# Decays of a Mamba-2 layer: four row-grouped exponents instead of six, y between the projections, past decays as a product, squares on ScalarE

## The chip, the cores and the metric

One core of a Trainium2 chip. The metric is the device time of one execution in microseconds (us), lower is better.

## The reference

A Mamba-2 mixer and a quantised feed-forward layer, both with a layer norm before and a residual after, over 4 x 256 tokens of width 512 in float32. Cut to what matters here:

```python
proj = einsum('bsd,ed->bse', x, in_proj_w)      # gate, hBC, dt
hBC = silu(conv4(hBC) + conv_b)                 # hs (128 heads x 64), B and C (8 groups x 128)
dt = clip(softplus(dt + dt_bias), 0, 100); A_dt = -exp(A_log) * dt
# two chunks of 128 tokens for each batch; A_cum is the cumulative sum of A_dt in a chunk
L = exp(segsum(A_dt))                           # own decays, below the diagonal
Y_diag = (C B^T * L) @ (hs * dt)                # inside a chunk
states = B^T (exp(A_cum_last - A_cum) * hs * dt)
Y_off = C @ prev_state * exp(A_cum)             # second chunk from the first
y = Y_diag + Y_off + hs * D
g = y * silu(gate); g = g * rsqrt(mean(g * g in its group) + eps) * norm_w
x = x + g @ out_proj_w.T
x = x + ffn(layernorm(x))                       # 1792 hidden, quantised activations
```

## The kernel before

Engines run their own programs and meet at semaphores; the order of the work on each is written out by hand. Matmuls that must be exact in float32 are split into high and low parts and done in three (`three`, L758 to L760).

**Outer order.** A prologue (norm of x, transposes, the projection of dt, softplus, cumulative sums, the first tile's and group's projections), then 8 groups of 8 tiles. A tile is two heads (128 channels) over all 1024 tokens. After the 8 tiles of a group comes a window: the B and C projections of the next group, the sum of squares, 16 blocks of out projection (L945 to L947) that are added to the residual, and the products of C and B (`cbs`, L840 to L842), kept masked in `cb`. The feed-forward layer follows.

**A step.** The step of tile t also makes the projections of tile t+1. On TensorE: transposes of half of `hs` (`turn`, L858), the exponents of two of six decay blocks (L867), `unit(0)` (12 matmuls of 128x512), the other transposes, two exponents, `unit(1)`, the first part of y (`y_first`, L881), the last two exponents, `unit(2)`, `unit(3)`, and `y_second` (L891). The blocks are: inside chunk 0, chunk 0 to chunk 1, and inside chunk 1, for each of two heads. An exponent is one bf16 matmul over 128 partitions, of which 15 hold rows (three parts of each cumulative sum, and marks); the rest are zeros.

ScalarE turns a block into a decay: for a block inside a chunk Relu and Exp in place in PSUM (L640, L644), for the past one Exp (L634). It also does the last tap of the convolution (`tap3`, L558), the tanhs (`hs_tanh` L569, `gate_tanh` L573), the scaling and upper part of the out weights (L666, L672), and the upper parts of the projection weights (L536).

VectorE multiplies decays by `cb` into `M` (`weigh`, L1163), turned hs by dt into `xdt` (`times_dt`, L1155), does the other three taps (`conv_rest`, L1068), the silus (L1082, L1087) and adds y (L1189). A projection bank comes free (`taken`) after `conv_rest` or after the gate's silu.

GpSimd makes the lower parts of weights (L406, L430), y times gate (`gated`, L438), its squares (L447; on ScalarE only in the very last tile, L679) and their sum (L452).

The SyncE queue loads, in each step and in this order, the out weights `wo_raw`, the rows of the next tile's exponents (four transfers) and the projection weights of the tile three pairs ahead (`load_pair`).

Of the kernel before, what the change touches and what calls it, by code (L numbers as in the profile page):

```python
# [12 lines left out]
P = 128  # L13
# [16 lines left out]
UNITS = 6  # L30
SLOT = [0, 1, 2, 3, 0, 1]
# [18 lines left out]
def over_tiles(eng, step, window):  # L50


    with eng.Fori(0, G - 1) as g:
        with eng.Fori(0, TPG // 2) as p:
            step(g, 2 * p, 0, True, True)
            step(g, 2 * p + 1, 1, True, True)
        window(g, True)
    with eng.Fori(0, TPG // 2 - 1) as p:
        step(G - 1, 2 * p, 0, True, True)
        step(G - 1, 2 * p + 1, 1, True, True)  # L60
    step(G - 1, TPG - 2, 0, True, False)
    step(G - 1, TPG - 1, 1, False, False)
    window(G - 1, False)
# [12 lines left out]
def mamba_ffn(nc, x, win, wdt, par, parbc, dt_bias, a_log, wout, w1, w3, w2, s1, s3, s2, out):  # L76
    rows_r = nc.dram_tensor("rows_r", (3, H, TOK), BF16, kind="Internal").ap()
    rows_l = nc.dram_tensor("rows_l", (3, B, H, 3, P), BF16, kind="Internal").ap()

    with ExitStack() as ctx:  # L80
# [23 lines left out]
        M = sb("M", [P, 4, HALF])  # L104
        bc = M[:, :, :].rearrange("p (a u) f -> p a (u f)", a=2)
# [3 lines left out]
        row_r = sb("row_r", [P, 2, 2, TOK], BF16)  # L109
        row_l = sb("row_l", [P, 2, 2, 3 * P], BF16)  # L110
        sq = sb("sq", [P, 2, HALF])
        after, bias_bc, nega_bc = [sq[:, 0, i * P:(i + 1) * P] for i in range(3)]
# [12 lines left out]
        qs = sb("qs", [P, 2, 4])  # L125
        qr = sb("qr", [P, 2, 4])
# [9 lines left out]
        rev, revrem = dte[:, 0:HALF], dte[:, HALF:TOK]  # L136
        r_part = flat[:, 4 * TOK:6 * TOK].bitcast(BF16)[:, 0:3 * TOK].rearrange("p (k f) -> p k f", k=3)
        neg_part = flat[:, 6 * TOK:8 * TOK].bitcast(BF16)[:, 0:3 * TOK].rearrange("p (k f) -> p k f", k=3)
        rev_part = pre[0].bitcast(BF16)[:, 0:3 * HALF].rearrange("p (k f) -> p k f", k=3)
# [3 lines left out]
        f_pair = M[:, :, :].rearrange("p k (w f) -> p w k f", w=2)  # L143
# [21 lines left out]
        diff = [bank("diff0"), bank("diff1")]  # L165
        ybank = [bank("y0"), bank("y1")]
        trb = bank("trb")
        misc = bank("misc")
        xbank = proj + diff
        nbank = [trb, misc]  # L170
        dbank = diff + [misc]
# [17 lines left out]
        s_held_p = sem("held_pool")  # L189
# [14 lines left out]
        s_part = [sem(f"exact_part{k}") for k in range(3)]  # L204
        s_rest = sem("rest_of_parts")
        s_rows = sem("rows_stored")
        s_raw = [sem("w_raw0_loaded"), sem("w_raw1_loaded")]
        s_rowq = [sem("rows_even_loaded"), sem("rows_odd_loaded")]
        s_out = sem("out_stored")
# [10 lines left out]
        turned = Tally(sem("hs_transposed"), 0, 2)  # L220
        xdts = Tally(sem("xdt_done"), 1, 2)
        dready = Tally(sem("diff_ready"), 0, UNITS)
        dbound = Tally(sem("diff_bounded"), 0, 4)
        edone = Tally(sem("exp_done"), 0, UNITS)
        mdone = Tally(sem("decay_done"), 3, UNITS)
        yready = Tally(sem("y_ready"), 1, 3)
# [47 lines left out]
        def _(sp):  # L274
# [12 lines left out]
            for n in range(3):  # L287
                load_pair(n, 2 * n if n else None)

            def load_rows(t, par_):  # L290
                sp.dma_start(row_r[0:3, par_, :, :], rows_r[:, bass.ds(2 * t, 2), :]).then_inc(s_rowq[par_], 16)
                for k in range(3):
                    sp.dma_start(row_l[3 + 4 * k:7 + 4 * k, par_, :, :].rearrange("b h f -> b (h f)"),
                                 rows_l[k, :, bass.ds(2 * t, 2), :, :].rearrange("b h q f -> b (h q f)"))\
                        .then_inc(s_rowq[par_], 16)


            for k in range(3):
                sp.wait_ge(s_part[k], 3)
                sp.dma_start(rows_r[k, :, :], r_part[:, k, :]).then_inc(s_rows, 16)  # L300
                sp.dma_start(rows_l[k, :, :, 1, :].rearrange("b h l -> h b l"),
                             rev_part[:, k, :].rearrange("h (b l) -> h b l", b=B)).then_inc(s_rows, 16)
                for z in range(2):
                    sp.dma_start(rows_l[k, :, :, 2 * z, :].rearrange("b h l -> h b l"),
                                 neg_part[:, k, :].rearrange("h (b z l) -> h z b l", z=2, b=B)[:, z, :, :])\
                        .then_inc(s_rows, 16)
            sp.wait_ge(s_const, 13)
            sp.dma_start(row_r[3:15, 0, 1, :], row_r[3:15, 0, 0, :]).then_inc(s_marks, 16)
            sp.dma_start(row_r[3:15, 1, 0, :], row_r[3:15, 0, 0, :]).then_inc(s_marks, 16)
            sp.dma_start(row_r[3:15, 1, 1, :], row_r[3:15, 0, 0, :]).then_inc(s_marks, 16)  # L310
            sp.wait_ge(s_rows, 16 * 12)
            load_rows(0, 0)

            def step(g, j, par_, nxt, nxt2):
# [39 lines left out]
        def _(pool):  # L354
# [18 lines left out]
            e.memset(row_r[:, :, :, :], 0.0).then_inc(s_const, 1)  # L373
            e.memset(row_l[:, :, :, :], 0.0).then_inc(s_const, 1)
            pool.wait_ge(s_const, 9)
            e.memset(row_l[0:3, :, :, :], 1.0).then_inc(s_const, 1)
            columns = row_r[:, 0, 0, :].rearrange("p (b f) -> p b f", b=B)
            for k in range(3):
                pool.wait_ge(s_const, 10 + k)
                e.affine_select(out=columns, in_=columns, compare_op=ALU.not_equal, fill=1.0, base=-3 - 4 * k,  # L380
                                pattern=[[-1, B], [0, S]], channel_multiplier=1).then_inc(s_const, 1)
# [31 lines left out]
            split_pair(0, 0)  # L413
            split_pair(1, 2)

            wholes = ((acum, rem, r_part), (rev, revrem, rev_part))
            for i, (whole, rest, parts) in enumerate(wholes):
                pool.wait_ge(s_part[0], i + 1)
                e.tensor_tensor(rest, whole, parts[:, 0, :], ALU.subtract).then_inc(s_rest, 1)
            for i, (whole, rest, parts) in enumerate(wholes):  # L420
                pool.wait_ge(s_rest, i + 1)
                pool.wait_ge(s_part[1], i + 1)
                e.tensor_tensor(parts[:, 2, :], rest, parts[:, 1, :], ALU.subtract).then_inc(s_part[2], 1)
            split_pair(1, 4)

            def step(g, j, par_, nxt, nxt2):
# [15 lines left out]
                for h in range(2 if nxt else 0):  # L442
# [74 lines left out]
        def _(act):  # L517
# [164 lines left out]
            def window(g, nxt):  # L682
# [24 lines left out]
                if not nxt:  # L707
                    x_upper(n2, TT - 3)
# [642 lines left out]
```

## Time and profile before

| | |
|---|---|
| median of 3 runs | 1861.39 us (1861.02 to 1861.64) |
| the profiled execution's own time | 1863.36 us |
| its span in the trace | 1861.6 us |
| granted TensorE clock, mean | 0.986 |
| PE, DVE, POOL, ACT busy | 97%, 67%, 54%, 49% |

PE is TensorE, PEld its weight loads, DVE VectorE, ACT ScalarE, POOL GpSimd. A busy share is that of the span in which at least one instruction of the engine is under way. Matmuls overlap their successors: what one costs in a stream is the distance between starts, not its duration. The same holds, more weakly, for DVE and ACT.

### The profile page before, as it was taken

The page shows a single profiled execution, that of the slowest core. Times are in us where ns is not written, and L with a number is a line of the kernel's source. Part 1 is how long each engine was busy: PE and PEld are TensorE (multiplying, and loading weights), DVE is VectorE, ACT ScalarE, POOL GpSimd, SP SyncE. Part 2 cuts the span into 40 slices and gives each one's busy share as a digit, 9 for nine tenths or more (in the row PEclk, how much of TensorE's full clock was granted, in tenths as well). Part 3 has the DMA queues.
Part 4 walks back from the last instruction along what each step waited for, and adds up shares of the span by engine and source line. Part 5 has one row for each costly group of instructions (what it writes and reads, how often), then busy time and mean ns, then how long its engine had stood idle before and what let it go on. Part 6 is the DMA issues. An engine that isn't in the chain of part 4 may idle for free.

```text
span 1861.6 us, 35838 instructions
## 1 busy us (share of the span) xinstructions
PE 1805.1 (97%) x10520; PEld 1448.8 (78%) x10520; DVE 1256.5 (67%) x2147; ACT 918.5 (49%) x1660; POOL 1006.2 (54%) x812
## 2 busy tenths in 40 slices
PE   5799999999999999999999999999999998999998
PEld 4577887788777877787778777887788776788886
DVE  6588728872887377746884688457754884877776
ACT  4466526652665256635663566346644663222221
POOL 4266645664566446654665366546654657633430
PEclk9899999999999999999999999999999997999999
DMA  2211101110111011101120111001101111111101
GB/s 93 63 53 41 46 3 45 52 52 0 47 53 52 0 47 51 53 0 36 46 64 6 29 53 53 17 29 53 47 23 30 42 35 53 40 52 35 51 17 46
DMA packets 49019, 74.94 MB, mean 40 GB/s; under 512 B 10356, under 2 KB 18676, under 8 KB 48984
## 3 DMA queue, kind: packets, MB, share of 16 engines
q1 hardware_dynamic: 47976, 73.12, 12.9%
q10 hardware_dynamic: 1008, 1.38, 0.2%
q8 instruction: 18, 0.29, 0.1%
q14 instruction: 17, 0.14, 0.0%
HBM read 70.35 MB, written 4.06 MB: 40 GB/s over the span
## 4 chain that ended last, share of the span: by engine, by line
PE 94%; DVE 2%; POOL 1%; issue 1%; ACT 1%; POOLq 0%; DVEq 0%; ACTq 0%
PE proj L758 16%; PE proj L760 16%; PE proj L759 16%; PE y L891 7%; PE y L945 6%; PE y L947 6%; PE y L946 6%; PE y L881 4%; PE trb L858 3%; PE diff L867 3%; PE y L758 2%; PE y L760 2%; PE y L759 2%; PE misc L867 1%; PE misc L931 1%
## 5 line engine op out<-in xcount | busy, mean ns | idle before, releaser
L758 PE MATMUL proj<-xhi,w_hi 128*128 128x512 f32 x1088 | 466.1, 428 | 5.4 <-DVE v L1068 5.4
L760 PE MATMUL proj<-xhi,w_lo 128*128 128x512 f32 x1088 | 426.2, 392 | 0.0
L759 PE MATMUL proj<-xlo,w_hi 128*128 128x512 f32 x1088 | 425.5, 391 | 0.0
L406 POOL TENSOR_TENSOR w_lo<-w_raw,w_hi 128x512 fp32r<-128x512 f32 x144 | 184.1, 1297 | 227.5 <-ACT w_hi L536 227.5
L1068 DVE SCALAR_TENSOR_TENSOR v<-proj,par_sb,v 128x510 f32<-128x510 f32 (+2 forms) x384 | 282.1, 742 | 14.9 <-ACT v L558 11.6
L758 PEld LDWEIGHTS proj<-xhi,w_hi 128*128 128x128 f32 x1088 | 205.0, 188 | 75.5 <-issue 7.9
L462 POOL TENSOR_TENSOR g_lo<-gated,g_hi 128x512 fp32r<-128x512 f32 x128 | 163.8, 1283 | 182.1 <-ACT g_hi L689 182.0
L760 PEld LDWEIGHTS proj<-xhi,w_lo 128*128 128x128 f32 x1088 | 204.8, 188 | 46.5
L759 PEld LDWEIGHTS proj<-xlo,w_hi 128*128 128x128 f32 x1088 | 205.4, 189 | 38.6
L1163 DVE TENSOR_TENSOR M<-diff,cb 128x512 f32<-128x512 f32 x256 | 170.4, 686 | 82.2 <-ACT diff L644 82.2
L945 PE MATMUL y<-wo_hi,g_hi 128*128 128x512 f32 x512 | 202.9, 396 | 4.0 <-POOL g_lo L462 4.0
L430 POOL TENSOR_TENSOR wo_lo<-wo_raw,wo_hi 128x512 f32 (+1 forms) x64 | 81.9, 1279 | 225.1 <-ACT wo_hi L672 225.1
L946 PE MATMUL y<-wo_lo,g_hi 128*128 128x512 f32 x512 | 200.1, 391 | 0.0
L947 PE MATMUL y<-wo_hi,g_lo 128*128 128x512 f32 x512 | 200.0, 391 | 0.0
L689 ACT CAST g_hi<-gated 128x512 fp32r<-128x512 f32 x128 | 78.6, 620 | 233.6 <-PE y L947 233.6
L558 ACT ACTIVATE v<-proj,par_sb 128x512 f32<-128x512 f32 x128 | 99.6, 778 | 188.7 <-PE proj L760 188.7
L1207 DVE SCALAR_TENSOR_TENSOR resid<-y,rg,resid 128x512 f32<-128x512 f32 x64 | 48.0, 750 | 201.3 <-PE y L947 171.5
L640 ACT ACTIVATE diff<-diff 128x512 f32<-128x512 f32 x192 | 105.5, 579 | 138.1 <-PE diff L867 138.1
L438 POOL TENSOR_TENSOR gated<-hs,gate 128x512 f32 (+1 forms) x128 | 162.8, 1295 | 1.6 <-DVE hs L1189 1.6
L452 POOL TENSOR_TENSOR sqacc<-sqacc,sq 128x512 f32<-128x512 f32 x128 | 163.1, 1297 | 0.0
L891 PEld LDWEIGHTS y<-M,xdt 128*64 128x64 f32 x2048 | 112.0, 138 | 25.7 <-issue 22.2
L891 PE MATMUL y<-M,xdt 128*64 128x128 f32 x2048 | 127.6, 278 | 2.5 <-DVE M L1163 2.5
(179 smaller groups left out, 3420.1 us busy)
## 6 DMA issues: line engine op xcount, KB each, us to landing
w_raw<-in_win SPq DMA_DIRECT2D x144, 256.0 KB, 2.7
wo_raw<-in_wout SPq DMA_DIRECT2D x64, 256.0 KB, 2.6
M<-in_w SPq DMA_DIRECT2D x14, 512.0 KB, 3.7
cb<-in_w SPq DMA_DIRECT2D x7, 512.0 KB, 3.4
row_l<-rows_l SPq DMA_DIRECT2D x192, 6.0 KB
out<-resid SPq DMA_DIRECT2D x8, 256.0 KB, 2.0
rows_l<-gated SPq DMA_DIRECT2D x9, 128.0 KB, 2.5
resid<-in_x SPq DMA_DIRECT2D x4, 256.0 KB, 4.7
```

What stands on the lines that cost most here:

```text
L406: e.tensor_tensor(w_lo[:, slot, i, :], w_raw[:, i, :], w_hi[:, slot, i, :].bitcast(F32), ALU.subtract).then_inc(split.sem, 1)
L452: e.tensor_tensor(halves(sqacc, h), halves(sqacc, h), sq[:, h, :], ALU.add)\
L462: e.tensor_tensor(g_lo[:, kk, :, :], gated[:, 4 * kk:4 * kk + 4, t * P:(t + 1) * P], g_hi[:, kk, :, :].bitcast(F32), ALU.subtract).then_in ...
L758: e.matmul(o, hi_l, hi_r, start=first, stop=False)
L759: e.matmul(o, hi_l, lo_r, start=False, stop=False)
L760: return e.matmul(o, lo_l, hi_r, start=False, stop=last)
L891: mm = e.matmul(ybank[b // 2][head * HD:(head + 1) * HD, (b % 2) * S + P:(b % 2 + 1) * S], xdt[:, 2 * b + part, head * HD:(head + 1) * HD] ...
L945: e.matmul(o, g_hi[:, kk, k, :], wo_hi[:, kt, :], start=first, stop=False)
L946: e.matmul(o, g_hi[:, kk, k, :], wo_lo[:, kt, :], start=False, stop=False)
L947: mm = e.matmul(o, g_lo[:, kk, k, :], wo_hi[:, kt, :], start=False, stop=last)
L1068: e.scalar_tensor_tensor(dst[:, :, d:S], src[:, :, 0:S - d], weights(K - 1 - d), dst[:, :, d:S], ALU.mult, ALU.add)\
L1163: e.tensor_tensor(M[:, SLOT[q], :], dbank[q % 3][:, :], cb[:, q // 2, :], ALU.mult)\
```

## The change

- **Exponents.** Four instead of six: only the blocks inside the chunks. Each one's 15 rows of both operands lie in their own group of 32 partitions (0, 32, 64, 96), and each writes its own PSUM bank: `row_r` and `row_l` shrink, and the rows are loaded with eight transfers instead of four. The exponents of tile j+1 are made in step j, behind y; those of a group's first tile in the window.
- **Decays.** `decay[z]` spans two banks, so Relu, Exp and `weigh_own` take both heads at once (128x1024). `trb` and `misc` become the banks of `decay[1]`; hs is turned into the y banks.
- **Past.** Chunk 0 to chunk 1 is a product. exp(A_cum) of the second chunk (`faded`) is made once, and two transfers in each step spread it over the partitions (`fade_l`); GpSimd multiplies it by `cb` (`weigh_past`, 128x1024). exp(A_last - A_cum) times dt (`fade_s`) is made once; `times_dt` multiplies hs by it as well (`xfade`, 128x512).
- **y.** One block of 24 matmuls between `unit(1)` and the exponents; all eight transposes stand in one block.
- **Squares.** On ScalarE in every tile, in one buffer, each half waiting for the sum of the half before; the last gate tanh of a step stands behind them.
- **Prologue.** B and C are projected before hs and gate of tile 0, with all four first units in banks of their own; fewer parts and rows are made; constants are smaller.

```diff
-            step(g, 2 * p, 0, True, True)
+            step(g, 2 * p, 0, True, True, True)
...
+        row_r = sb("row_r", [P, 2, HALF], BF16)
+        row_l = sb("row_l", [P, 2, P], BF16)
+        fade_l = sb("fade_l", [P, 2, HALF])
+        fade_s = sb("fade_s", [P, B, H])
+        xfade = sb("xfade", [P, B, P])
+        sq = sb("sq", [P, HALF])
...
+        decay = [ctx.enter_context(nc.psum_tensor(f"decay{z}", [P, 2 * HALF], F32)) for z in range(2)]
+        diff = [decay[0][:, 0:HALF], decay[0][:, HALF:2 * HALF]]
+        ypair = ctx.enter_context(nc.psum_tensor("y", [P, 2 * HALF], F32))
+        misc, trb = decay[1][:, 0:HALF], decay[1][:, HALF:2 * HALF]
```

SyncE, one step:

```diff
                 if nxt:
-                    sp.wait_ge(dready.sem, dready.at(g, j, 1))
+                    sp.wait_ge(dready.sem, dready.at(g, j, 0))
                     load_rows(TPG * g + j + 1, 1 - par_)
+                    sp.wait_ge(pdone.sem, pdone.at(g, j, 1))
+                    load_fade(TPG * g + j + 1)
```

GpSimd, the constants:

```diff
-            e.memset(row_r[:, :, :, :], 0.0).then_inc(s_const, 1)
-            e.memset(row_l[:, :, :, :], 0.0).then_inc(s_const, 1)
+            e.memset(row_r[0:PARTS + PARTS * B, :, :], 0.0).then_inc(s_const, 1)
+            e.memset(row_l[:, :, :], 1.0).then_inc(s_const, 1)
```

GpSimd, the past decays and the squares:

```diff
+            def weigh_past(g, j):
+                pool.wait_ge(s_fade, (32 * TPG) * g + 32 * j + 32)
+                pool.wait_ge(cbd.sem, cbd.at(g, 0, 0))
+                pool.wait_ge(yready.sem, yready.at(g, j, 0))
+                e.tensor_tensor(M[:, 4:6, :], fade_l[:, :, :], cb[:, 1:2, :].broadcast_to([P, 2, HALF]), ALU.mult)\
+                    .then_inc(pdone.sem, 1)
...
-                for h in range(2 if nxt else 0):
-                    ...
-                    e.tensor_tensor(sq[:, h:h + 1, :], one, one, ALU.mult).then_inc(sqs.sem, 1)
+                if ahead:
+                    weigh_past(g, j + 1)
```

ScalarE, the order of a step after:

```diff
+                if nxt:
+                    tap3(0, w, ready.at(g, j, 1), silu.at(g, j, -1))
+                if nxt2:
+                    upper_pair(par_, 9 * g + j + 3)
+                if nxt:
+                    tap3(1, w, ready.at(g, j, 2), silu.at(g, j, 0))
+                    hs_tanh(hs[:, 1 - par_, :], 0, taken.at(g, j, 1))
...
+                if ahead:
+                    bounded(g, j + 1, 0)
+                if nxt:
+                    hs_tanh(hs[:, 1 - par_, :], 1, taken.at(g, j, 2))
+                if ahead:
+                    bounded(g, j + 1, 1)
+                    exponential(g, j + 1, 0)
+                if nxt:
+                    gate_tanh(gate[:, 1 - par_, :], 0, ready.at(g, j, 3))
+                if ahead:
+                    exponential(g, j + 1, 1)
+                for h in range(2):
+                    act.wait_ge(gdone.sem, gdone.at(g, j, h + 1))
+                    act.wait_ge(sacc.sem, sacc.at(g, j, h))
+                    e.activation(sq[:, :], gated[...], ACT.Square).then_inc(sqs.sem, 1)
+                if nxt:
+                    gate_tanh(gate[:, 1 - par_, :], 1, ready.at(g, j, 4))
```

TensorE:

```diff
+            def exponents(g, j, par_):
+                pe.wait_ge(mdone.sem, mdone.at(g, j, 0))
+                pe.wait_ge(s_rowq[par_], (TPG * 64) * g + 64 * j + (128 - 64 * par_))
+                pe.wait_ge(cbd.sem, cbd.at(g, 0, 0))
+                for z in range(2):
+                    for head in range(2):
+                        first = 32 * (2 * z + head)
+                        mm = e.matmul(decay[z][:, head * HALF:(head + 1) * HALF],
+                                      row_l[first:first + PARTS + PARTS * B, par_, :],
+                                      row_r[first:first + PARTS + PARTS * B, par_, :], start=True, stop=True)
+                    mm.then_inc(dready.sem, 1)
...
                 if nxt:
                     unit(0)
-                turn(1)
-                exponents(2)
-                exponents(3)
+                turn()
                 if nxt:
                     unit(1)
-                y_first()
-                exponents(4)
-                exponents(5)
+                y()
+                if ahead:
+                    exponents(g, j + 1, 1 - par_)
                 if nxt:
                     unit(2)
                     unit(3)
-                y_second()
```

VectorE, the order of a step after:

```diff
+                times_dt()
+                if nxt:
+                    conv_rest(0, w, tap.at(g, j, 1), convs.at(g, j, 0))
+                    conv_rest(1, w, ..., (lambda: hs_silu(hs[:, 1 - par_, :], 0, tanh.at(g, j, 1)),))
...
+                if nxt:
+                    hs_silu(hs[:, 1 - par_, :], 1, tanh.at(g, j, 2))
+                if ahead:
+                    weigh_own(g, j + 1, 0)
+                if nxt:
+                    gate_silu(gate[:, 1 - par_, :], 0, tanh.at(g, j, 3))
+                if ahead:
+                    weigh_own(g, j + 1, 1)
+                if nxt:
+                    gate_silu(gate[:, 1 - par_, :], 1, tanh.at(g, j, 4))
```

## Rows read from the trace of the kernel before

**Rows 1.** The page: busy time of each engine, share of the span, instructions.

```profile
PE 1805.1 (97%) x10520; PEld 1448.8 (78%) x10520; DVE 1256.5 (67%) x2147; ACT 918.5 (49%) x1660; POOL 1006.2 (54%) x812
```

**Rows 2.** Timeline of PE, a step: start us, us to the last's end, what.

```profile
703.69 1.97 PE L891 MATMUL y<-M,xdt 128*64 128x128 f32 x32
705.58 0.66 PE L858 MATMUL trb<-ident,hs 128*128 128x128 f32 x4
706.08 0.59 PE L867 MATMUL diff<-row_r,row_l 128*128 128x512 bf16 x2
...
712.97 1.09 PE L881 MATMUL y<-M,xdt 128*64 128x128 f32 x16
714.00 0.39 PE L867 MATMUL diff<-row_r,row_l 128*128 128x512 bf16 x1
...
714.67 0.40 PE L759 MATMUL proj<-xlo,w_hi 128*128 128x512 f32 x1
...
720.03 1.97 PE L891 MATMUL y<-M,xdt 128*64 128x128 f32 x32
```

**Rows 3.** Timeline of PE, the C and B products of a window.

```profile
828.37 0.38 PE L840 MATMUL diff<-M 128*128 128x128 f32 x2
...
830.82 0.39 PE L842 MATMUL misc<-M 128*128 128x128 f32 x2
```

**Rows 4.** Timeline of DVE and ACT in a step.

```profile
708.09 1.29 DVE L1163 TENSOR_TENSOR M<-diff,cb 128x512 f32<-128x512 f32 x2 [0.82 <-ACT diff L644]
...
715.50 1.52 DVE L1068 SCALAR_TENSOR_TENSOR v<-proj,par_sb,v 128x508 f32<-128x508 f32 x2
```

```profile
706.49 1.07 ACT L640 ACTIVATE diff<-diff 128x512 f32<-128x512 f32 x2 [1.59 <-PE diff L867]
...
714.22 0.63 ACT L569 ACTIVATE hs<-v 128x512 f32<-128x512 f32 x1 [0.16 <-DVE v L1068]
```

**Rows 5.** Groups by line and shape: busy us, mean ns, idle before.

```profile
L666 ACT ACTIVATE wo_raw<-wo_raw,par_sb 128x512 f32<-128x512 f32 x64 | 47.1, 736 | 0.0
...
L712 ACT CAST w_hi<-M 128x1024 fp32r<-128x1024 f32 x8 | 8.3, 1043 | 0.7 <-POOL M L497 0.7
...
L679 ACT ACTIVATE sq<-gated 128x512 f32<-128x512 f32 x2 | 1.3, 629 | 4.8 <-POOL gated L438 4.8
```

```profile
L1110 DVE SCALAR_TENSOR_TENSOR gated<-gated 128x1024 f32<-128x1024 f32 x1 | 1.2, 1226 | 0.0
```

**Rows 6.** Groups of POOL by line and shape.

```profile
L438 POOL TENSOR_TENSOR gated<-hs,gate 128x512 f32 x124 | 157.8, 1295 | 0.0
L447 POOL TENSOR_TENSOR sq<-gated 128x512 f32 x124 | 126.7, 1046 | 0.0
...
L501 POOL TENSOR_TENSOR w_lo<-M,w_hi 128x1024 fp32r<-128x1024 f32 x8 | 19.2, 2402 | 52.4 <-ACT w_hi L712 52.4
```

**Rows 7.** DMA issues, the page: KB each, us from issue to landing.

```profile
w_raw<-in_win SPq DMA_DIRECT2D x144, 256.0 KB, 2.7
```

**Rows 8.** Timelines of POOL, DVE and PE in the prologue.

```profile
2.62 3.51 POOL L373 MEMSET row_r<- 128x4096 bf16 x1
```

```profile
39.67 2.31 DVE L1068 SCALAR_TENSOR_TENSOR v<-proj,par_sb,v 128x510 f32<-128x510 f32 x3
...
45.13 1.22 DVE L1119 SCALAR_TENSOR_TENSOR gated<-dt,sq 128x1024 f32<-128x1024 f32 x1
```

```profile
42.13 0.77 PE L758 MATMUL proj<-xhi,w_hi 128*128 128x512 f32 x1 [4.29 <-DVE v L1068]
...
76.43 0.77 PE L840 MATMUL diff<-M 128*128 128x128 f32 x2 [11.14 <-DVE M L1082]
...
84.45 0.49 PE L758 MATMUL proj<-xhi,w_hi 128*128 128x512 f32 x1
```

**Rows 9.** Timeline of PE, from the last projections to the last window.

```profile
1532.59 1.97 PE L891 MATMUL y<-M,xdt 128*64 128x128 f32 x32
...
...
1552.69 3.55 PE L931 MATMUL misc<-ones,sqacc 128*128 128x1 f32 x16 [4.73 <-POOL sqacc L452]
```

More of the change, by code:

```diff
@@ L285, in load_pair @@
                     sp.dma_start(w_raw[:, i, :], win[n, i, :, :]).then_inc(s_raw[i], 16)
-            for n in range(3):
-                load_pair(n, 2 * n if n else None)
+            for k, n in enumerate((1, 0, 2)):
+                load_pair(n, 2 * k if k else None)
             def load_rows(t, par_):
[L291 to L295, printed above, removed]
@@ new lines, in load_fade @@
+            def load_fade(t):
+                for head in range(2):
+                    sp.dma_start(fade_l[:, head, :], faded[bass.ds(2 * t + head, 1), :]
+                                 .rearrange("a f -> (a f)").partition_broadcast(P)).then_inc(s_fade, 16)
+            sp.wait_ge(s_const, 12)
+            for q in range(1, 4):
+                sp.dma_start(row_r[32 * q + PARTS:32 * q + PARTS + PARTS * B, :, :],
+                             row_r[PARTS:PARTS + PARTS * B, :, :]).then_inc(s_marks, 16)
@@ new lines, in _ @@
+            sp.wait_ge(s_fade_l, 2)
+            sp.dma_start(faded, faded_sb).then_inc(s_faded, 16)
+            for k in range(PARTS):
+                sp.wait_ge(s_part[k], 1)
+                for z in range(2):
+                    sp.dma_start(rows[:, z, k, :, :],
+                                 parts[:, k, :].rearrange("h (b z l) -> h z b l", b=B, z=2)[:, z, :, :])\
+                        .then_inc(s_rows, 16)
+            sp.wait_ge(s_faded, 16)
+            load_fade(0)
+            sp.wait_ge(s_rows, 32 * PARTS)
@@ L312, in _, with step @@
             load_rows(0, 0)
-            def step(g, j, par_, nxt, nxt2):
+            def step(g, j, par_, nxt, nxt2, ahead):
                 sp.wait_ge(wolo.sem, wolo.at(g, j, 0))
@@ L648, in step, with exponential, decays @@
+            def exponential(g, j, z):
+                act.wait_ge(dbound.sem, dbound.at(g, j, z + 1))
+                e.activation(decay[z][:, :], decay[z][:, :], ACT.Exp, scale=-1.0).then_inc(edone.sem, 1)
+            def decays(g, j):
+                bounded(g, j, 0)
+                bounded(g, j, 1)
+                exponential(g, j, 0)
+                exponential(g, j, 1)
+            decays(0, 0)
+            def step(g, j, par_, nxt, nxt2, ahead):
                 w = tile_weights(TPG * g + j + 1)
@@ L706, in window @@
                             x_upper(n2, (i - 7) // 2)
+                if nxt:
+                    decays(g + 1, 0)
                 if not nxt:
@@ L879, in y_first @@
                     for b in range(B):
-                        for head in range(2):
-                            mm = e.matmul(ybank[b // 2][head * HD:(head + 1) * HD, (b % 2) * S:(b % 2) * S + P],
-                                          xdt[:, 2 * b, head * HD:(head + 1) * HD],
-                                          M[:, SLOT[head], b * P:(b + 1) * P], start=True, stop=True)
-                    mm.then_inc(yready.sem, 1)
-                def y_second():
-                    pe.wait_ge(mdone.sem, mdone.at(g, j, 6))
-                    for b in range(B):
-                        for part in range(2):
+                        cols = slice(b * P, (b + 1) * P)
@@ L954, in window @@
                         turn_x(n2, t - 2, hs[:, t % 2, 0:HID])
+                    if i == 13 and nxt:
+                        exponents(g + 1, 0, 0)
             over_tiles(pe, step, window)
@@ L1115, in _ @@
             link(e.scalar_tensor_tensor(dtq, dtv, 0.0, dtq, ALU.max, ALU.add))
+            for h in range(2):
+                hs_silu(bc[:, 0, :], h, h + 1)
             dt_flat = dt[:, :, :].rearrange("p t f -> p (t f)")
@@ L1179, in step @@
-                weigh(4)
-                weigh(5)
+                own = tile_weights(t)
+                for h in range(2):
+                    dve.wait_ge(yready.sem, yready.at(g, j, h + 1))
+                    e.scalar_tensor_tensor(halves(y, h), halves(y, h), own(K + 1), ybank[h][:, :],
+                                           ALU.mult, ALU.add).then_inc(ysum.sem, 1)
                 if nxt:
                     hs_silu(hs[:, 1 - par_, :], 1, tanh.at(g, j, 2))
+                if ahead:
+                    weigh_own(g, j + 1, 0)
```

390 lines of the change are left out of this document (170 added, 220 removed).

## The prediction

> **What bounds the kernel now.** I read the busy shares first: PE stands at 97%, DVE at 67%, no other engine above 54% [rows 1]. Then the timeline of one step of PE. From one second block of y to the next are 16.34 us [rows 2], and PE never waits in between, so a step is worth what PE's stream costs. Its terms are distances between starts. Two exponents and one unit matmul take 0.67 us (714.00 to 714.67), with 0.23 for the unit matmul 0.22 for each exponent. From 714.44, where unit 2 begins, to y at 720.03 two units take 5.50 us and about 0.09 passes before y starts: 2.75 a unit. y costs 1.03 us with 16 records and 1.89 with 32, so 0.054 a record and 0.17 a block. Four transposes cost 0.50 behind y; spread over 0.66 with 0.27 for one, they are 0.11 to 0.13 each. The sum is 11.0 + 1.03 + 1.89 + 2 x 0.09 + 0.95 + 6 x 0.22 = 16.37. The prologue's timeline shows where PE is not full: 4.3 us before the third unit, 11.1 before the C and B products, a first step's unit at 84.45 [rows 8]. The tail does too: from the last unit (its end is the start of y, 1532.6) to the last window are 20.1 us, 4.7 of them a wait [rows 9].
>
> **The step on PE.** Removed are two exponents, 0.44 us. y becomes one block: 0.17 + 0.09 = 0.26 less. The other four exponents are 0.88 if they still run one after another and 0.22 if all run at once. The trace has a case of matmuls in separate parts of the array: the two heads of y go to the lower and upper 64 output partitions, and their records are 0.054 apart. The products of C and B, with the same 128 columns in float32 but the full array, take 22 records from 828.37 to 830.82, 0.111 apart [rows 3]. So different column groups overlap already, two at a time. Row groups are nowhere in the trace; I take overlap, near the 0.22 end, since here the operands don't even share partitions. A change of the array's division costs something: the bound is nothing below and one block's 0.26 above, and I take 0.25, as two changes now stand around the exponents. PE's step is then 11.0 + 0.95 + (0.09 + 0.17 + 48 x 0.054 = 2.85) + 0.22 + 0.25 = 15.25 us; without overlap 15.9.
>
> A rule of the Trainium skill speaks against part of this: TensorEngine Tiling (Array Packing), Key Properties, says that changing the tiling mode drains the TensorE. The trace agrees as far as y's fixed 0.17 + 0.09 goes. TensorE: Matmul & The Clock Gate, Part 3, gives 3.07 times for four row groups, which would make 0.88 into 0.29 us, an estimate 0.07 above mine.
>
> **Will the others keep up?** They did at 16.34; at 15.25 the order of ACT and DVE matters. Prices: a 512-wide op on DVE every 0.60 (1.29 for two, 0.69 for one), a dependent tap every 0.76; ACT every 0.49 to 0.54 with 0.58 to 0.63 to its end [rows 4]. A 1024-wide op is 1.04 on ACT and 1.23 on DVE by the nearest rows [rows 5]; from PSUM I take 1.0 and 1.22, and the next may start 0.07 earlier. I follow one step from unit 0's start at 0. Unit 0 ends at 2.75, eight transposes at 3.7, and `times_dt` starts at 3.9: 1.14 for xdt, 0.60 for xfade. conv 0 runs 5.7 to 7.95. `hs_tanh(0)` starts 0.1 later, as in rows 4, at 8.05; then ACT runs the scaled weights (8.6, 0.77 as 0.74 plus a hop [rows 5]), `wo_hi` (9.4), `bounded(0)` at 9.9 (the exponents are out by 9.8), `hs_tanh(1)` at 10.9 (conv 1 with a silu in it ends at 10.83), `bounded(1)` 11.5, `exponential(0)` 12.4 to 13.4, gate tanh 0 to 13.9. DVE waits for the exponential, weighs until 14.6, and only then is the silu of gate 0: bank free at 15.27. With 0.15 for PE (41.98, the taps' end, to 42.13 [rows 8]) the next unit 0 starts at **15.42**, 0.17 after PE would be ready. So the bound of a step turns from PE into this chain, and the forecast is 15.4: 0.94 us less in each of 63 steps, **59 us**. What was once queued behind PE is now ahead of it; were these hops free, the gain would be 63 x 1.1 = 69.
>
> The other waits stay hidden. Squares cost POOL 2 x 1.05 before; `weigh_past` costs 2.4 (2.6 as two halves of 1.3 above; half of that, if the repeated operand is cheap, below) [rows 6]. So POOL's step is unchanged, 11.5 us of 15.4. The squares on ACT (0.63 each [rows 5]) wait for `gated`, and the second for the sum of the first: y added at 11.5, gated to 12.8 and 14.05, square 0 behind `exponential(1)` to 15.4, sum to 16.7, square 1 to 17.35, gate tanh 1 to 17.9, its silu to 18.6. Unit 1 of the next step needs that bank at 15.4 + 3.7 = 19.1, so with 0.15 for PE 0.35 us is all the cover; anything later stops unit 1, and behind it y and the next exponents. The second sum ends at 18.7 and `weigh_past` at 21.1; y needs it at 15.4 + 6.5 = 21.9. Transfers: 512 KB more in a step beside 768; a 256 KB one lands in 2.7 us [rows 7], the fade is asked for at about 6 and used 13 us later. `load_pair` now stands behind it, and lands near 10, used at 19. Eight row transfers instead of four take the queue about 3 us of 15, hidden as well. The tables of ScalarE don't change: the square of the last tile ran without a load.
>
> **Prologue.** The memset of `row_r` has a quarter of its 4096 columns: 2.6 of 3.51 us gone ahead of the norm's roots [rows 8]; I take 2. The first two units then end at 35.7, and units 2 and 3 have banks of their own, so there is no 4.3 us wait; six units end at 46.8. dt is later on DVE: 46.35 - 2 + 2.3 (second conv before it) + 1.2 (two silus) = 47.9. Sums to 50.5, C's taps end at 52.5, the last unit at 56. On ACT the parts and fades stand behind C's tanh: 53.2, five operations, then hs's tap at 57.6, and DVE's taps end at 62.3. The C and B products begin at 62.4 instead of 76.43, and if the 8.0 us from there to the step's first unit stay, it starts at 70.4: **14 us** less. The rows are a near rival in time: parts 61.2, stored by 64.5, loaded by 69.5.
>
> **Tail.** With its decays made ahead, the last tile has transposes, y, the sum, the products: gate silu 3.5 us after the last unit, xdt and xfade 1.9, y 2.9 to 5, y added 0.8, and gated, sum, square, sum 5.8 behind: about 15 instead of 20.1. **5 us** less.
>
> **Sum.** 59 + 14 + 5 = 78. The profiled execution took 1863.4 us, its span 1861.6; the median is 1861.4, so its terms are 0.1% off at most. 1861.4 - 78 = 1783 us.
>
> **Rivals.**
> (1) Row groups don't overlap, the change does less than it says: PE's step 15.9 instead of 15.4, 63 x 0.44 + 19 = 47 less, 1815. For it: no row shows it. Against: y's pairs overlap.
> (2) The chain is shorter than I count (hops, wide ops): PE bounds at 15.1 to 15.25, 63 x 1.15 + 22 = 94 less, 1767.
> (3) The chain is longer. Four wide ops stand on it; at 0.12 us more each the step is 15.9, at 0.2 more 16.2: 1815 to 1833.
> (4) Slower: the past decays come late, since POOL's wide product of `fade_l` and a repeated `cb` costs w instead of 2.4 us. y waits for it on PE, with the exponents and two units queued behind. A y later by s makes the step longer by s, which gives POOL s more as well: 18.7 + w + 0.15 = 15.4 + s + 6.5 + s, so s = (w - 3.0) / 2. Nothing is lost up to 3.0; the step passes 16.65, where prologue and tail no longer pay for it, at w = 5.5. At 6.5 the step is 17.15: 1861 + 63 x 0.81 - 19 = 1893. For it: POOL has no such operation in the trace. Against: its 1024-wide product costs 2.4, under twice its 512-wide one [rows 6].
> (5) No difference: the gain in the step eaten exactly; 1860.
>
> **Chances.** The forecast 0.52, its own range 1772 to 1798. (1) 0.13, (2) 0.17, (3) 0.12, (4) 0.04, (5) 0.02. The range must take in (2) and most of (1) and (3): 1762 to 1820. Faster by over 0.2% (what a measurement of this kernel tells from nothing, 3.7 us): 0.94; within 0.2% 0.02; slower 0.04.
>
> **What would show it.** Starts of the four exponents within 0.1 us of each other; 15.4 us between two y; PE's waits led by DVE's gate silu before unit 0, about 0.2 us in most steps; unit 0 of the first step near 70; the last window's product 15 us after the last unit; PE's busy share about 96%. I am wrong if PE waits elsewhere (y for `weigh_past`, unit 1 for the second gate, exponents for rows), or if exponents stand 0.22 apart.

## The result and the profile after

The changed kernel takes 2107.45 us (median of 4, 2107.06 to 2108.59) and the kernel before 1861.2: a ratio of 1.132 (1.130 to 1.134). That is 246 us slower, where 78 us faster were forecast. Its span is 2106.0 us at a granted clock of 0.942 (before 0.986).

The page, the busy shares (answers to [rows 1]):

```profile
PE 1837.3 (87%) x10392; PEld 1472.5 (70%) x10392; DVE 1268.5 (60%) x1892; ACT 911.7 (43%) x1399; POOL 1055.5 (50%) x747
```

No engine is full any more, and none has more work in its busy time that could explain 246 us (PE 32 more, DVE 12, POOL 49, ACT 7 less). So this is a wait. Who waits, in the view of waits (engine, line, releaser: us in total, times, longest):

```profile
POOL w_lo L426 <- ACT w_hi L561: 403.3, 64, 8.0
ACT w_hi L561 <- DMA w_raw<-in_win: 380.3, 57, 7.4
...
PE proj L784 <- DVE v L1087: 205.5, 55, 4.5
```

and the load queue's own waits:

```profile
SPq L314 <- POOL M L449: 761.9, 62, 60.8
```

PE waits for VectorE's taps, and ScalarE's cast of the projection weights waits for their transfer. What is late is the load `w_raw`, which no step of the forecast had as late. Line 314 is `load_fade`: SyncE stands there until `weigh_past` has read the old fade. The page's rows of transfers (KB each, us from issue to landing) show what comes on top:

```profile
w_raw<-in_win SPq DMA_DIRECT2D x144, 256.0 KB, 4.2
fade_l<-faded SPq DMA_DIRECT2D x128, 256.0 KB, 3.9
```

The same load took 2.7 us before [rows 7]. The chain of work that ended last, one turn of a step (start us, us, what), closes a ring, a loop of waits that leads from one step's product to the next one's:

```profile
806.23 2.40 POOL M L449
808.78 0.36 SPq L314
...
809.99 4.33 DMA w_raw<-in_win
814.34 0.62 ACT w_hi L561 x2
...
815.45 0.78 ACT v L583
...
818.03 0.74 DVE v L1087
...
819.46 1.41 DVE hs L1212 x2
...
821.78 1.72 POOL gated L466
...
824.08 1.30 POOL sqacc L473
...
827.50 2.41 POOL M L449
```

Read it from the first M (`weigh_past`) to the next, 21.27 us later. M 2.40; 1.36 until SyncE has issued the fade and then `load_pair`; 4.35 until `w_raw` lands; 1.11 for ScalarE's casts, for `upper_pair` stands ahead of `tap3(1)` in its order; 4.01 through the second convolution on VectorE to the y sum; 4.04 through that sum and `gated`; 0.58, the first square; 3.42 for the sums and the second square; and `weigh_past` again. TensorE is not in it, nor in the turns next to it (from 757 to 851 us the chain has no matmul). It waits for the bank that the second convolution frees: the timelines of ACT and PE around that turn (in brackets the idle time before and its releaser):

```profile
814.34 1.21 ACT L561 CAST w_hi<-w_raw 128x512 fp32r<-128x512 f32 x2 [6.29 <-DMA w_raw<-in_win]
```

```profile
798.34 0.80 PE L784 MATMUL proj<-xhi,w_hi 128*128 128x512 f32 x1 [3.92 <-DVE v L1087]
798.93 0.63 PE L785 MATMUL proj<-xlo,w_hi 128*128 128x512 f32 x1
799.36 0.63 PE L786 MATMUL proj<-xhi,w_lo 128*128 128x512 f32 x1
...
806.66 1.03 PE L903 MATMUL y<-ident,hs 128*128 128x128 f32 x8
807.45 0.48 PE L784 MATMUL proj<-xhi,w_hi 128*128 128x512 f32 x1
...
810.38 0.44 PE L919 MATMUL y<-M,xdt 128*64 128x128 f32 x4
...
813.15 0.40 PE L885 MATMUL decay<-row_r,row_l 15*128 15x512 bf16 x4
813.47 0.50 PE L784 MATMUL proj<-xhi,w_hi 128*128 128x512 f32 x1
813.81 0.39 PE L785 MATMUL proj<-xlo,w_hi 128*128 128x512 f32 x1
...
819.60 0.50 PE L784 MATMUL proj<-xhi,w_hi 128*128 128x512 f32 x1 [3.11 <-DVE v L1087]
```

Behind the 3.92 us wait that ends at 798.34 the matmuls start 0.43 apart instead of 0.23, and the stretches show the low level, 1.2 GHz, being granted part of the time, then the high one, 2.4 GHz, again (columns: stretch, its us, busy time of each engine, PEclk, share of DMA, GB/s):

```profile
797.00:801.00 4.00, 2.66 (x6) 2.15 (x7) 3.96 (x5) 3.48 (x5) 2.98 (x3) 0.54 0.26 67
...
805.00:810.00 5.00, 5.00 (x27) 4.19 (x27) 2.85 (x4) 1.17 (x2) 3.62 (x2) 1.00 0.02 7
```

That goes with the waits (0.992 is granted where they are gone, below), but not with each of them: behind the 3.11 us wait that ends at 819.60 the granted clock stays 1.00. As TensorE is not in the ring, the clock is no cause of its length. The excerpt also has three of the forecast's terms: the transposes take 0.79 (806.66 to 807.45), y 2.77 (810.38 to 813.15), and the four exponents, which are one row. The four of them last 0.40 together, about what one lasts, and delay the next matmul by 0.32 and the one behind it by 0.11 more (813.47 to 813.81 instead of 0.23), so 0.43.

### The profile page after: what moved, and what is told of

Read it like the earlier page. It is cut to its first block, busy times and chain, and to the rows that moved or that the text cites. A ratio compares the mean times of both kernels' runs of the same rounds, so it can differ in the third digit from the quotient of the medians.

```text
span 2106.0 us, 34523 instructions
## 1 busy us (share of the span) xinstructions
PE 1837.3 (87%) x10392; PEld 1472.5 (70%) x10392; DVE 1268.5 (60%) x1892; ACT 911.7 (43%) x1399; POOL 1055.5 (50%) x747
## 4 chain that ended last, share of the span: by engine, by line
PE 37%; issue 17%; POOL 15%; DMA 11%; DVE 10%; ACT 4%; SPq 3%; POOLq 1%; DVEq 1%; ACTq 1%
DMA w_raw<-in_win 11%; POOL M L449 6%; PE y L964 5%; PE y L966 5%; PE y L965 5%; POOL gated L466 5%; DVE v L1087 4%; PE proj L784 4%; PE proj L786 4%; PE proj L785 4%; POOL sqacc L473 4%; DVE hs L1212 3%; SPq L314 2%; ACT v L583 2%; PE y L784 1%
## 5 line engine op out<-in xcount | busy, mean ns | idle before, releaser
L785 PE MATMUL proj<-xlo,w_hi 128*128 128x512 f32 x1080 | 457.7, 424 | 0.0
L786 PE MATMUL proj<-xhi,w_lo 128*128 128x512 f32 x1080 | 455.5, 422 | 0.0
L1087 DVE SCALAR_TENSOR_TENSOR v<-proj,par_sb,v 128x510 f32<-128x510 f32 x378 | 280.0, 742 | 280.6 <-ACT v L583 259.8
L561 ACT CAST w_hi<-w_raw 128x512 fp32r<-128x512 f32 x144 | 87.7, 620 | 381.4 <-DMA w_raw<-in_win 380.3
L466 POOL TENSOR_TENSOR gated<-hs,gate 128x512 f32 (+1 forms) x128 | 190.0, 1506 | 55.8 <-DVE hs L1212 55.8
L919 PE MATMUL y<-M,xdt 128*64 128x128 f32 x2048 | 170.6, 277 | 4.9 <-POOL M L449 4.9
L1101 DVE SCALAR_TENSOR_TENSOR hs<-hs,v 128x512 f32<-128x512 f32 x128 | 166.2, 1298 | 1.0
L449 POOL TENSOR_TENSOR M<-fade_l,cb 128x1024 f32<-128x1024 f32 x64 | 153.5, 2398 | 2.9 <-issue 2.9
L1178 DVE TENSOR_TENSOR M<-decay,cb 128x1024 f32<-128x1024 f32 x128 | 154.3, 1211 | 0.5 <-ACT decay L659 0.5
L1106 DVE SCALAR_TENSOR_TENSOR gate<-gate,proj 128x512 f32<-128x512 f32 x128 | 86.9, 679 | 104.6 <-ACT gate L598 104.6
```

The source lines that it names most:

```text
L449: e.tensor_tensor(M[:, 4:6, :], fade_l[:, :, :], cb[:, 1:2, :].broadcast_to([P, 2, HALF]), ALU.mult)\
L466: e.tensor_tensor(gated[:, bass.ds(j, 1), h * HALF:(h + 1) * HALF], hs[:, par_:par_ + 1, h * HALF:(h + 1) * HALF], gate[:, par_:par_ + 1, ...
L785: e.matmul(o, hi_l, lo_r, start=False, stop=False)
L786: return e.matmul(o, lo_l, hi_r, start=False, stop=last)
L919: mm = e.matmul(ybank[b // 2][head * HD:(head + 1) * HD, (b % 2) * S + z * P:(b % 2) * S + (z + 1) * P], inputs[:, head * HD:(head + 1) * ...
L1087: e.scalar_tensor_tensor(dst[:, :, d:S], src[:, :, 0:S - d], weights(K - 1 - d), dst[:, :, d:S], ALU.mult, ALU.add)\
```

## The experiments

All are edits of the changed kernel, numbered e1 to e10 as the expectations name them. Times are medians of 4 runs with an interval of the ratio to before, or of a single run where no interval is given (e2, e3); before took 1861.1 to 1862.4 beside them.

**The pair first (e1).** In the step of the load queue:

```diff
+                if nxt2:
+                    load_pair(9 * g + j + 3, split.at(g, j, 0))
                 if nxt:
                     sp.wait_ge(dready.sem, dready.at(g, j, 0))
                     load_rows(TPG * g + j + 1, 1 - par_)
                     sp.wait_ge(pdone.sem, pdone.at(g, j, 1))
                     load_fade(TPG * g + j + 1)
-                if nxt2:
-                    load_pair(9 * g + j + 3, split.at(g, j, 0))
```

> Theory A, a ring through the load queue: in the changed kernel the projection weights of a step are asked for behind the wait on the past decays' product (end of it at 808.63, w_raw issued 809.99, landed 814.34), ScalarE casts them in the same step ahead of the second tap, and from there the second convolution, y's sum, gated, squares and sums lead back to the next product: 21.3 us a turn. With load_pair ahead of the rows and the fade in the queue's step the weights are there in time, and a step falls from 20.4 to 15.4 to 16.2 us: 1785 to 1840 us. ScalarE's wait for w_raw, 380 us now, is under 20. Rival B, contention: silus of hs take 1.30 us in the mean instead of 0.69 and gated 1.51 instead of 1.30 where VectorE and GpSimd run at the same time, and these make the steps long whatever the queue does: over 2040. Rival C, the traffic of the fade itself (w_raw lands in 4.2 us instead of 2.7): it remains, over 2000.

Measured 1816.49 us, ratio 0.976 (0.974 to 0.977): 291 us come back with two lines moved, all that the change had lost and 45 more. ScalarE's wait for `w_raw` is gone, the clock is 0.992. The edit also moves the load ahead of the wait for the exponents' rows; the queue's view of waits in the changed kernel names only the one for `weigh_past` there.

The starts of the exponents show where the 291 us lay. The first two distances behind a window are the same in both kernels, 15.13 and about 16.0 us; the other five of a group are 21.25 in the mean instead of 15.89, and the stretch over a window 87.4 instead of 76.5. So the ring closes anew in each group, behind its second step.

Most of the 33 us between this run and the forecast can be seen in a step; timelines of DVE, ACT, POOL and PE:

```profile
720.00 0.69 DVE L1101 SCALAR_TENSOR_TENSOR hs<-hs,v 128x512 f32<-128x512 f32 x1
...
723.36 1.58 DVE L1101 SCALAR_TENSOR_TENSOR hs<-hs,v 128x512 f32<-128x512 f32 x1
724.87 1.21 DVE L1178 TENSOR_TENSOR M<-decay,cb 128x1024 f32<-128x1024 f32 x1
```

```profile
719.33 0.63 ACT L594 ACTIVATE hs<-v 128x512 f32<-128x512 f32 x1 [0.75 <-DVE v L1087]
...
723.64 0.97 ACT L659 ACTIVATE decay<-decay 128x1024 f32<-128x1024 f32 x1
```

```profile
723.11 2.99 POOL L466 TENSOR_TENSOR gated<-hs,gate 128x512 f32 x2 [0.30 <-DVE hs L1212]
...
730.10 2.40 POOL L449 TENSOR_TENSOR M<-fade_l,cb 128x1024 f32<-128x1024 f32 x1
```

```profile
710.89 0.50 PE L784 MATMUL proj<-xhi,w_hi 128*128 128x512 f32 x1 [0.59 <-DVE gate L1106]
...
717.50 0.44 PE L919 MATMUL y<-M,xdt 128*64 128x128 f32 x4
...
726.73 0.50 PE L784 MATMUL proj<-xhi,w_hi 128*128 128x512 f32 x1 [0.39 <-DVE gate L1106]
```

The same silu of hs costs 0.69 alone and 1.58 beside `gated`, which itself takes 2.99 for two instead of 2 x 1.30 [rows 6]. It stands on the chain to `gate_silu(0)`, and TensorE waits for that before unit 0 in every step (30.1 us, 63 times). But only part of it counts: the weighing behind it starts 0.26 us after its Exp ends (724.87 against 724.61). The chain was late before: the first tanh starts 8.44 us after unit 0 (719.33 against 710.89), where the forecast has 8.05.

**The pair's cast late (e2).** The queue is as the change has it; ScalarE casts the pair behind `tap3(1)` and the first tanh of hs:

```diff
-                if nxt2:
-                    act.wait_ge(ready.sem, ready.at(g, j, 0))
-                    upper_pair(par_, 9 * g + j + 3)
                 if nxt:
                     tap3(1, w, ready.at(g, j, 2), silu.at(g, j, 0))
                     act.wait_ge(gdone.sem, gdone.at(g, j, 0))
                     hs_tanh(hs[:, 1 - par_, :], 0, taken.at(g, j, 1))
+                if nxt2:
+                    act.wait_ge(ready.sem, ready.at(g, j, 0))
+                    upper_pair(par_, 9 * g + j + 3)
```

> Only ScalarE's order goes back: the weights are cast behind the second tap and the first tanh of hs, as in the kernel before; the load queue is as in the changed kernel. Theory A: the ring stays but takes the next way: product, fade and weights 5.7 us, casts, scaled out weights, decays, squares and sums, some 19 to 20 us a turn, so 1990 to 2090 us. If the place of the casts alone is the cause (the load being late but harmless): 1785 to 1850.

Measured 2025.3 us (a single run). Only 82 us: the ring stays and takes GpSimd's queue instead, where the pair's `w_lo` stands ahead of `wo_lo` and `gated` and all three run back to back (the chain, start us and us; a piece is the part of an operation that lies on it):

```profile
820.24 0.68 POOL w_lo L426
...
822.75 0.09 POOL wo_lo L458
...
824.00 2.96 POOL gated L466 x2
```

From one `weigh_past` to the next are 19.4 us here (811.56 to 830.95), as expected.

**The fade without its traffic (e3).** In the step `load_fade` fills one partition instead of 128 (so the past decays of all but the first tile are wrong on the other 127); every wait stays.

```diff
-            def load_fade(t):
+            def load_fade(t, n=1):
...
-                    sp.dma_start(fade_l[:, head, :], faded[bass.ds(2 * t + head, 1), :]
-                                 .rearrange("a f -> (a f)").partition_broadcast(P)).then_inc(s_fade, 16)
+                    sp.dma_start(fade_l[0:n, head, :], faded[bass.ds(2 * t + head, 1), :]
+                                 .rearrange("a f -> (a f)").partition_broadcast(n)).then_inc(s_fade, 16)
```

> The fade's two transfers of a step are still issued at their place behind the wait, but carry one partition instead of 128, so the past decays are those of the first tile on the other 127: the waits and the issues stay, the traffic goes. Theory A: w_raw lands in 2.7 instead of 4.2 us, a step loses 1.5 us, 63 steps 95 us: 1990 to 2030 us. Rival C, traffic as the cause: 1785 to 1850.

Measured 2006.07 us (a single run). The load lands in 2.7 us again:

```profile
ACT w_hi L561 <- DMA w_raw<-in_win: 289.7, 68, 5.5
...
w_raw<-in_win SPq DMA_DIRECT2D x144, 256.0 KB, 2.7
```

So the traffic of the spread rows is worth 101 us. The 95 expected were 1.5 in each of 63 steps, and that it came out so near is in part luck: the first two steps of a group lose nothing, the other five 1.85 in the mean (21.25 to 19.40), and the stretch over a window 4.0. The landing is 1.5 of each 1.85; the two spreads are also issued in 0.23 us each instead of 0.36. What is left, 190 of the 291, goes with the wait and the issues ahead of the load, which this run keeps.

**The gate's chain short (e4).** From here on the pair is first. Both orders changed at once: on ScalarE the out weights ahead of hs's first tanh and both Relus and the first Exp ahead of its second (shown), on VectorE the second silu of hs behind `gate_silu(0)`:

```diff
                 if ahead:
                     bounded(g, j + 1, 0)
-                if nxt:
-                    hs_tanh(hs[:, 1 - par_, :], 1, taken.at(g, j, 2))
-                if ahead:
                     bounded(g, j + 1, 1)
                     exponential(g, j + 1, 0)
+                if nxt:
+                    hs_tanh(hs[:, 1 - par_, :], 1, taken.at(g, j, 2))
```

> On top of e1. There a step is 15.8 us, and TensorE waits 0.4 to 0.6 us for the silu of gate 0 before unit 0. Theory: the chain of ScalarE and VectorE before that silu sets it. Here ScalarE scales and casts the out weights before the first tanh of hs, and makes the second Relu and the first Exp before the second tanh; VectorE makes the second silu of hs behind the gate's silu. The gate's silu should come 1 us earlier, ahead of TensorE's need at 15.3: 30 us of waits and some of their restarts go, 1779 to 1792 us. Rival: the step is bound elsewhere (unit 1 by the squares' ring, y by the past decays' product): within 6 us of e1's 1816.

Measured 1836.69 us, ratio 0.986 (0.985 to 0.988): 20 us worse than the pair alone, where 24 to 37 better were expected. Here unit 1 waits for the second gate's silu as well: from the transposes to unit 1 are 1.33 us (722.49 to 723.82) instead of 0.79. Each order was then run by itself.

**VectorE's order only (e5).**

```diff
-                if nxt:
-                    hs_silu(hs[:, 1 - par_, :], 1, tanh.at(g, j, 2))
...
+                    hs_silu(hs[:, 1 - par_, :], 1, tanh.at(g, j, 2))
```

> On top of e1, only VectorE's order: the second silu of hs behind the gate's silu. In e1 this silu takes 1.6 instead of 0.69 us while GpSimd multiplies gated, and the weighing behind it starts at 724.87, 0.2 us after its Exp is done (724.61). So 0.2 us a step: 1801 to 1811 us. If VectorE's slowed silu were all of the stall: about 1785.

Measured 1807.34 us, 0.971 (0.969 to 0.972). The silu's mean is 731 ns instead of 1115, and TensorE's wait for the gate 12.1 us instead of 30.1. The time fell by 9, as the 0.2 us a step had it, not by 18: the trace has unit 1 start 0.90 us after the transposes in most steps now instead of 0.79, 6 us in all.

**ScalarE's order only (e6).** The same ScalarE order as in the run of both, VectorE's as in the change.

> On top of e1, only ScalarE's order. Theory: VectorE's second silu of hs still stands ahead of the weighing, its tanh now comes 1.4 us later, it runs against gated on GpSimd and takes 1.6 us: the gate's silu comes 0.9 us later than in e1, 1850 to 1880 us. Rival: VectorE and GpSimd don't slow one another, the stretched silu waits for something else: the gate's silu at the same time or earlier, 1785 to 1820.

Measured 1888.5 us, 1.014 (1.012 to 1.016). The direction was expected, the size was 8 us over the range. Both silus of a step now meet GpSimd; DVE and POOL:

```profile
723.79 1.59 DVE L1101 SCALAR_TENSOR_TENSOR hs<-hs,v 128x512 f32<-128x512 f32 x1
...
736.76 1.47 DVE L1101 SCALAR_TENSOR_TENSOR hs<-hs,v 128x512 f32<-128x512 f32 x1 [0.45 <-ACT hs L594]
```

```profile
723.54 2.96 POOL L466 TENSOR_TENSOR gated<-hs,gate 128x512 f32 x2 [2.97 <-DVE hs L1212]
...
736.40 1.28 POOL L458 TENSOR_TENSOR wo_lo<-wo_raw,wo_hi 128x512 f32 x1 [1.62 <-ACT wo_hi L684]
```

With the out weights scaled and cast early, hs's first tanh comes behind them and `wo_lo` falls under its silu. That silu stands ahead of the y sum in VectorE's order, so `gated` starts 13.5 us after unit 0 (723.54 against 710.06) instead of 12.2 (723.11 against 710.89). TensorE waits 89.0 us for the gate. The run of both has the same early cast and the same late `gated`, and with it late squares, which stand ahead of the second gate's tanh.

**The squares on GpSimd (e7, e8).** The pair first, and the squares of all tiles but the last where they were before the change; then the same with VectorE's order:

```diff
+                        e.tensor_tensor(sq[:, :], one, one, ALU.mult).then_inc(sqs.sem, 1)
...
-                for h in range(2):
+                for h in range(0 if nxt else 2):
```

> On top of e1, the squares of all tiles but the last go back to GpSimd. Its step grows from 11.5 by 2.1 us to some 14 of 15.8, still under the step; the past decays' product then ends about where y needs it. 1815 to 1835 us. If the ring of squares and sums between ScalarE and GpSimd held the step in e1: below 1812.

Measured 1813.6 us, 0.974 (0.972 to 0.976), 3 us below the pair alone, where it was to be at most 1.5 below; the two intervals overlap. The steps behind the second are 15.89 us in the mean in both; the stretch over a window is 75.8 instead of 76.5.

> e5 and e7 together, on top of e1: VectorE's second silu of hs behind the gate's silu, squares on GpSimd. e5 left 12 us of waits for gate 0 of e1's 30, e7 20. If the two act apart, e5's 1807 less e7's 3 us: 1800 to 1806 us. If GpSimd's longer step now runs against the moved silu: 1808 to 1820.

Measured 1803.78 us, 0.969 (0.968 to 0.971). This is what both taken apart would give. Now y waits for `weigh_past` 41 times, 12.5 us in all.

**The decays before the second tanh (e9).** To the last kernel, on ScalarE:

```diff
-                if nxt:
-                    hs_tanh(hs[:, 1 - par_, :], 1, taken.at(g, j, 2))
-                if ahead:
                     bounded(g, j + 1, 1)
                     exponential(g, j + 1, 0)
+                if nxt:
+                    hs_tanh(hs[:, 1 - par_, :], 1, taken.at(g, j, 2))
```

> e8, and ScalarE makes both Relus and the first Exp before the second tanh of hs (the out weights stay where they are, so that their product on GpSimd doesn't meet the first silu of hs, as it did in e4). The first Exp comes 0.5 us earlier, so gate 0's silu is ahead of TensorE's need: the 12 us of waits and their restarts go, 1785 to 1797 us. If another wait takes its place (unit 1, y): 1798 to 1812.

Measured 1804.33 us, 0.970 (0.968 to 0.971): nothing gained, as its rival said, for TensorE's wait moved to y:

```profile
PE y L925 <- POOL M L450: 35.4, 55, 4.9
```

**The same, the squares on ScalarE (e10),** as the change has them:

> As e9, but the squares stay on ScalarE as in the change. With the gate's second tanh behind the ring of squares and sums, unit 1 may wait, as it did in e4: 1790 to 1815 us, at least 3 us above e9. If the place of the squares doesn't matter: within 3 us of e9.

Measured 1785.98 us (1784.83 to 1786.57), 0.960 (0.958 to 0.961): the best of all. It was expected at least 3 us above the last and is 18 below. Two products fewer on GpSimd let `weigh_past` end ahead of y:

```profile
PE y L918 <- POOL M L449: 4.7, 1, 4.7
```

This one is in the tail. One wait in its steps is not in that view. Timelines of PE and DVE:

```profile
636.73 1.04 PE L902 MATMUL y<-ident,hs 128*128 128x128 f32 x8
...
637.90 0.50 PE L783 MATMUL proj<-xhi,w_hi 128*128 128x512 f32 x1
```

```profile
637.16 0.69 DVE L1105 SCALAR_TENSOR_TENSOR gate<-gate,proj 128x512 f32<-128x512 f32 x1 [1.61 <-ACT gate L598]
```

From the transposes to unit 1 are 1.17 us instead of 0.79: unit 1 starts as the second gate's silu ends (637.85). The modelled end of the transposes covers most of it, so only the distance of starts shows it. Over the whole run it is 10 us, in 32 of 63 steps. Between exponents are 15.12 us (705.13 to 720.25) where unit 1 doesn't wait and 15.63 (627.99 to 643.62) where it does.

## Why the prediction was wrong

**The step that failed** is the last about transfers: "the fade is asked for at about 6 and used 13 us later. `load_pair` now stands behind it, and lands near 10, used at 19." Its landing time was right (814.34, 10.7 us after that step's unit 0 at 803.62). Its use was not: the pair that a step loads is cast in the same step, and the change had moved that cast ahead of `tap3(1)`. With the pair first, ScalarE casts 4.15 us after unit 0's start (730.88 against 726.73); in the changed kernel it stood ready at 808.05 and the load landed at 814.34. I took the queue's order into account and not ScalarE's. The second half is that a late use there is not a stall once but a ring: everything between the cast and `weigh_past` is behind it, and the load is behind `weigh_past`. Shown by moving the load (291 us), by moving the cast (the ring shifts, 82 us) and by removing the traffic (101 us). The rivals held a late `weigh_past` for y, none a load behind its wait; the chance of slower, 0.04, was far too small.

**Mis-sized: the chain to `gate_silu(0)`.** The sum had 15.42 for the step. With the pair first it is 15.8 to 16.0 (704.23 to 720.27 is 16.04, 720.27 to 736.08 is 15.81). Two terms make it. Unit 0, the transposes and conv 0 bring the first tanh to 8.44 instead of 8.05: the transposes start 2.89 us after unit 0 instead of 2.75 (710.89 to 713.78), and conv 0 takes the rest. And the second silu of hs, which the sum had hidden behind the Exp, takes 1.58 beside `gated` and delays the weighing by 0.26; moving it gave back 9 us of the 33. Once no silu meets GpSimd and the Relus are ahead of the tanh, the step is 15.12 or 15.63.

**Right, point by point.**
- Row groups overlap: in the trace the four starts lie within 0.02 us. By the forecast's own measure (two exponents and a unit matmul 0.67) four and a unit matmul take 0.66 (813.15 to 813.81), so 0.43 for the four and what changes around them, forecast 0.22 + 0.25 = 0.47; serial would have been 0.88 or more. Rival (1) falls.
- y's block 2.77 against 2.85; eight transposes 0.79 against 0.95. In the best kernel a step without a wait is 15.12 us against the 15.25 of TensorE's stream.
- Wide operations: Relu and Exp 0.97 to 1.03 (forecast 1.0), `weigh_own` 1.21 (1.22), `weigh_past` 2.40 (2.4). Rivals (3) and (4), which asked these to be longer, fall in their reasons. But the result that (3) gave for a longer chain, 15.9 us and 1815, is what the pair first shows, by other terms.
- GpSimd's ring: with the pair first, `weigh_past` ends 5.8 us after unit 0's start (forecast 21.1 - 15.4 = 5.7) and y comes at 6.6 (6.5).
- "0.35 us is all the cover" of unit 1: used up in every other step of the best kernel.
- Prologue and tail in their totals; the ring does not touch them. Timeline of PE in the changed kernel:

```profile
67.42 0.79 PE L784 MATMUL proj<-xhi,w_hi 128*128 128x512 f32 x1
```

```profile
1781.83 1.03 PE L903 MATMUL y<-ident,hs 128*128 128x128 f32 x8
1787.78 0.69 PE L919 MATMUL y<-M,xdt 128*64 128x128 f32 x4 [4.92 <-POOL M L449]
...
1797.54 1.62 PE L950 MATMUL decay<-ones,sqacc 128*128 128x1 f32 x7 [5.55 <-POOL sqacc L473]
```

The first unit stands at 67.42 instead of 84.45 [rows 8], 17.0 less (forecast 14); from the last unit to the last window are 15.7 us instead of 20.1 [rows 9], 4.4 less (5). In the tail the path was another: the last y waits 4.92 us for `weigh_past`, a wait that the forecast's sum for the tail does not name, so that the total fits is in part luck.

In the best kernel 1392.2 us lie between the first unit and the end of the last (67.53 to 1459.72), before 1448.1 [rows 8, 9]: 55.9 less, forecast 59. It ends 75 us below before, against 78. That is a kernel with other orders in the queue, on VectorE and on ScalarE than the forecast was worked out for. With the queue's order alone put right it is 45 us below before, not 78. So the forecast sized what the change can give, and did not see that its own queue order loses 291 us, nor that its orders on the two engines hold the step 0.5 us longer than it counted.

Open: how the 190 us divide between the wait and the issues ahead of the load, and why conv 0 takes longer than counted. A second buffer for the fade, which should also break the ring, was not tried.

## What to carry to other kernels

When a transfer that must wait for a buffer joins a queue, list what stands behind it and look up the consumer of each in its own engine's order, in the same turn; if that consumer leads back to the wait, the ring's whole length becomes the step, however idle each engine is. The mark of it here: the chain view of the steps (806 to 851 us) is led by "issue" (27.8%) and a transfer (19.3%), while every engine's busy share falls. Move the load that nobody has to wait for ahead of the wait; and before a product is put on GpSimd, or an operation moved in VectorE's order, see which operations of VectorE with two operands in SBUF will run beside it.

## What the runs showed of the hardware

**VectorE and GpSimd hold each other up.** Groups of the changed kernel:

```profile
L466 POOL TENSOR_TENSOR gated<-hs,gate 128x512 f32 (+1 forms) x128 | 190.0, 1506 | 55.8 <-DVE hs L1212 55.8
...
L1101 DVE SCALAR_TENSOR_TENSOR hs<-hs,v 128x512 f32<-128x512 f32 x128 | 166.2, 1298 | 1.0
```

The silu of hs reads two operands in SBUF. Its mean is 687 ns before, 1298 here, 1115 with the pair first, 1484 with ScalarE's order, 731 with VectorE's and 719 in the best kernel, whose `gated` is back at 1295 ns too. VectorE's operations that read PSUM beside the same products keep their length (`weigh_own` 1.21). The Trainium skill, SBUF — State Buffer, Who interferes with whom, says that a VectorE instruction with two SBUF inputs contends with a GpSimd one that reads SBUF. The same page of the Trainium skill, SBUF: two separate sides, calls the shared pair of ports an exclusive lock that goes to whichever starts first, for the whole instruction. The trace agrees: alone a silu of hs takes 0.68 to 0.69 us, and one that starts inside an operation of GpSimd ends 0.54 to 0.56 us after that operation ends, whenever it started (118 silus of the changed kernel, 63 with the pair first, 126 with ScalarE's order). With ScalarE's order the product ends at 737.68 and the silu, started at 736.76, at 738.23; with both orders (e4) they end at 720.04 and 720.59, and the silu, started at 719.46, takes 1.13. What GpSimd starts meanwhile grows too (`sqacc` 1.75 instead of 1.29 at 719.99 in e4). The forecast looked at what GpSimd costs and not at what runs beside it.

**Row groups.** Four matmuls of 15 rows and 512 columns in four groups of partitions, each into its own bank, start within 0.02 us of each other and cost the stream 0.43 us with what changes around them, where one over all 128 partitions cost 0.22 [rows 2].

**Spread rows.** Two transfers that spread a row over 128 partitions, 256 KB each, land in 3.9 us (3.3 with the pair first, where no load of the pair stands right behind them) and delay the loads asked for right behind them from 2.7 to 4.2; with one partition's worth of traffic it is 2.7 again.
